# Order of the sums, the transposes and the right logits in each TensorE slot of an edge stage

## What is computed

```python
feat_src_e = feat_all[edge_type, edge_src]          # a gathered row of 256 features per edge
el = sum(feat_src_e * attn_l[edge_type])            # left logit, 4 heads
er = sum(feat_dst_e * attn_r[edge_type])            # right logit, from the destination's tile
e = leaky_relu(el + er)
ex = exp(e - segment_max(e, edge_dst)[edge_dst])    # softmax over the edges of a node
alpha = ex / segment_sum(ex, edge_dst)[edge_dst]
h = segment_sum(alpha[..., None] * feat_src_e, edge_dst)
```

## Time and profile before

| | us |
|---|---|
| median of 3 runs | 2175.03 (2172.45 to 2175.23) |
| profiled execution | 2174.1 |
| its span, first to last instruction | 2172.0 |
| first gather starts | 258.71 |
| last gather starts | 1512.77 |
| last addition of the edge stage starts | 1563.22 |

### The profile page before, as it was taken

How to read it: one execution, slowest core, us unless ns; L and a number is a source line. 1 busy time by engine, 2 the same in 40 slices (tenths; PEclk the granted TensorE clock), 3 DMA queues, 4 the chain that set the end, 5 groups by cost and what they waited for, 6 DMA issues and landing times. The chain is left out here.

```text
span 2172.0 us, 38726 instructions
## 1 busy us (share of the span) xinstructions
PE 1840.9 (85%) x9090; PEld 1554.6 (72%) x9091; DVE 1137.2 (52%) x3066; ACT 850.6 (39%) x2220; POOL 1140.9 (53%) x1130
## 2 busy tenths in 40 slices
PE   7999867888888887988888888887552999999998
PEld 6888766766767776766766766676352888888887
DVE  4333145767666677767767676776773121212121
ACT  2222354444444454544544544542083222222222
POOL 4000177777777777777777777776056122222222
PEclk9999857788788798888888888887855999999999
DMA  6443344444444444444444444443144777777764
GB/s 222 167 188 143 142 112 110 112 114 112 110 113 110 111 112 112 112 113 109 112 113 110 112 112 110 112 108 97 44 161 150 233 218 234 222 224 223 227 217 130
DMA packets 120198, 308.99 MB, mean 142 GB/s; under 512 B 26951, under 2 KB 70855, under 8 KB 105828
## 3 DMA queue, kind: packets, MB, share of 16 engines
q0 software_dynamic: 60192, 149.24, 26.7%
q1 hardware_dynamic: 59844, 158.18, 21.3%
HBM read 250.66 MB, written 57.71 MB: 142 GB/s over the span
## 5 line engine op out<-in xcount | busy, mean ns | idle before, releaser
L716 POOL DMA_INDIRECT gath<-feats,idxT x996 | 951.7, 956 | 512.6 <-issue 295.0
L1014 PE MATMUL psP<-gath,hot 128*128 128x260 f32 x1992 | 614.1, 462 | 50.7 <-DVE gath L825 49.9
L1014 PEld LDWEIGHTS psP<-gath,hot 128*128 128x128 f32 x1992 | 435.0, 230 | 135.3 <-issue 47.7
L1001 PEld LDWEIGHTS psE<-er,hotT 128*128 128x128 f32 x1992 | 294.8, 227 | 122.4 <-issue 121.4
L1001 PE MATMUL psE<-er,hotT 128*128 x1992 | 309.1, 304 | 79.3 <-issue 37.7
L937 ACT COPY hotT<-psOT 128x512 f32<-128x512 f32 x249 | 144.9, 582 | 453.5 <-PE psOT L985 453.2
L927 ACT ACTIVATE hot<-cst,ndlT 128x128 f32<-128x128 f32 x996 | 317.5, 393 | 6.5 <-PEq L307 6.5
L834 DVE TENSOR_TENSOR acc<-acc,psP 128x260 f32 x498 | 210.2, 422 | 195.8 <-PE psP L1014 76.0
L1536 POOL DMA_INDIRECT out<-yrow,node x66 | 102.6, 1555 | 390.9 <-DVE yrow L1651 292.5
L825 DVE TENSOR_TENSOR gath<-gath,psA 128x1024 f32<-128x1024 f32 x249 | 301.1, 1219 | 9.9 <-ACT gath L957 2.5
L1606 ACT ACTIVATE hT<-psH,w1buf 128x256 f32<-128x256 f32 (+1 forms) x320 | 119.1, 434 | 352.2 <-PE psH L1566 352.2
(11 more groups left out here) (224 smaller groups left out, 1192.9 us busy)
## 6 DMA issues: line engine op xcount, KB each, us to landing
w1buf<-in_experts SPq DMA_DIRECT2D x40, 1030.0 KB, 7.8
w2buf<-in_experts SPq DMA_DIRECT2D x40, 1024.0 KB, 5.4
feats<-frow SPq DMA_DIRECT2D x30, 1040.0 KB, 4.0
gath<-feats,idxT POOLq DMA_INDIRECT x996
meta<-in_edges SPq DMA_DIRECT2D x464, 12.0 KB
xrow<-slots_x SPq DMA_DIRECT2D x26, 258.0 KB, 6.4
b_all<-in_b SPq DMA_DIRECT2D x40, 128.0 KB, 6.5
xs<-xb SPq DMA_DIRECT2D x5, 768.0 KB, 10.0
```

The source lines that it names most:

```text
L716: pool.indirect_dma_start(gath[:, r, u], None, feats, bass.IndirectOffsetOnAxis(ap=idxT[:, r, u:u + 1], axis=0)).then_inc(gath_in[r], 16)
L1001: ins = pe.matmul(psE[:, u * W % 512:u * W % 512 + W], hotT[:, j % 2, k * P:(k + 1) * P], tables[k // BLK], start=True, stop=True)
L1014: ins = pe.matmul(psP[:, bank(g, b, r), 0:FW], hot[:, r, u], gath[:, r, u], start=u % BLK == 0, stop=u % BLK == BLK - 1)
```

## The change

In each slot the call of `total` moves from the end to the start. Nothing is added or removed; the once-a-group work, and the order on all other engines, stay where they are. Before, a slot is transposes, right logits, sums; now it is sums, transposes, right logits.

```diff
                     def slot(s):
+                        if s < SLOTS_Q - LAG:
+                            total(g - 1, (r - 1) % GBUFS, s + LAG)
+                        else:
+                            total(g, r, s - (SLOTS_Q - LAG))
                         if s + 2 < SLOTS_Q:
                             turn(g + 1, (r + 1) % GBUFS, s + 2)
                         else:
...
                             right_logits(g + 1, s + 1)
                         if s == 5 and there(g + AHEAD):
                             meta_rows(g + AHEAD)
-                        if s < SLOTS_Q - LAG:
-                            total(g - 1, (r - 1) % GBUFS, s + LAG)
-                        else:
-                            total(g, r, s - (SLOTS_Q - LAG))
```

## The result

The changed kernel takes 2216.26 us (median of 4 runs, 2205.66 to 2221.23) against 2175.13 before (median of 4 runs taken with it): a ratio of 1.0187, 95% interval 1.0171 to 1.0204. It is slower by 41 us, where 2237 had been forecast. Its profiled execution took 2212.11 us, 38 more than the one of before, and its span is 2210.1 us.

The account below looks back on a forecast made before the run. POOL's gathers were taken to pace the edge stage at 40.3 us a group; 0.4 + 1.1 + 1.2 = 2.7 us a period, 2.3 beyond the slack, gave 63 us on 2174.1: 2237, range 2174 to 2268.

Parts of the forecast that it names:

- the slack: Edge stage: TensorE and VectorE alone take 39.9 us against POOL's pace of 40.3, so 0.4 us a period is hidden.
- Place C: `pick_right(g+1,1)`, which needs quad 7's right logits, now behind the sums of quad 1: 1.2 us a period.
- high-clock end of 0.3: Low end of the 0.3 to 1.0 us price at the pick of quad 7's right logits, TensorE at high clock.
- low-clock end of 3.4: Price at the pick of quad 7's right logits if TensorE runs at the low clock: 3.4 us.
- Place B: Ahead of L1059: transposes and right logits now come between quad 6's sums and L1059; 1.1 us a period.
- 0.35 us case: Ahead of L1059: the price if the clock has risen again by the transposes and right logits, 1.25 - 0.9.
- Place A: Ahead of L1050 and `pick_right(g+1,0)`: delay behind the sums of quad 4, set against a gain; +0.4 us a period.
- gain weighed against it: Sums of quad 3 no longer wait 1.01 us, so VectorE's wait for L1050 may shrink by up to 0.9 us a period.
- The last two periods: End of the edge stage, without POOL's cover: 5.4 us more, less 4.9 us that group 30 waited for its gather.
- range of 8 in 10: Whole kernel: the time was to lie between 2174 and 2268 us.
- case held most likely: Whole kernel: the forecast case, 2205 to 2262 us, given a chance of 0.52.
- The rival that followed the Trainium skill: TensorE's clock: short holes leave it alone, the low clock does not spread; 1.05 us a period, 2189 us, chance 0.16.

## Why the prediction was right, and where it was off

**What bounds the kernel: right.** POOL paces the stage and the slack is 0.4 us a period. The kernel with fewer gathers has an own period of 40.0 us, and every full kernel with an own period up to 40.6 us came out within 0.2% of before. (A slip without consequence: POOL's row of sevens begins with the sixth slice, not the fifth.)

**Place C, the pick of right logits: right in kind, too small.** 1.2 us a period were taken, 1.7 were measured as a wait, and 2.0 as the effect of slot 6 on top of the others. The high-clock end of 0.3 came out: 6.7 us in 27 periods with the holes filled. The low-clock end of 3.4 never came; the longest wait is 1.9, since the clock falls for the sums and rises again for the transposes. That "new holes of up to a microsecond" would appear was too little; the hole is 1.7 to 2.2 us in all periods but one. About 1.3 us of it are the transposes and right logits that now stand behind the sums. Another 0.8 is a wait ahead of the right logits of slot 4 that is gone. The trace names no cause for it; two register loads stand there, and they now run while sums are queued ahead. Such waits came to 35.0 us before and are gone from the list. TensorE's timeline of before has this one:

```profile
792.15 1.07 PE L1001 MATMUL psE<-er,hotT 128*128 x8 [0.83 <-issue]
```

**Place B, L1059: right in kind, too large.** 1.1 us were taken, 0.7 measured. The sums of quad 6 do run at the low clock (3.83 us), but in the period shown the clock rises before the transposes and right logits behind them are through, which is the 0.35 us case of the text and a part of the next. On top of the other seven slots it does not lengthen the own period.

**Place A, L1050: the number came out, the gain did not come where it was looked for.** The wait for L1050 is 0.4 us a period longer, as taken. But the gain weighed against it, up to 0.9 us off that same wait, did not come. A gain of 0.6 came at another place, VectorE's waits ahead of additions (L834), which had no term in the sum. The kernel with slots 0, 1 and 2 alone has it (122.6 down to 106.9 us) and those with slot 3 or slot 6 alone hardly (118.8 and 123.0), so it belongs to the early slots.

**The sum.** 2.7 us a period were forecast and 2.0 measured, so beyond the slack 1.6 x 27 = 43 us came instead of 62. What is off is mostly the gain ahead of additions, which had no term; place B, too large by 0.4, and place C, too small by 0.5, cancel, and that is luck. The last two periods were to cost 0.5 us net and gave 6.1: 4.9 for the wait, as priced, and 2.1 in period 30 (1563.05 - 1529.55 against 1526.14 - 1490.54), less 0.9 by which period 29 is longer without its wait. Period 30 has transposes and right logits for a short group only; that this is why it is shorter was not tried. 43.0 - 6.1 is 37, against 63 forecast. The measured 2216 lies in the range of 8 in 10 and in the case held most likely.

**A step that failed** without consequence: POOL was to be held back at the end. It never was, with a delay of 43 us, just over one period, and three buffers. So two of the signs named, a POOL that waits longer than 0.3 us for sums and a later last gather, did not come. The others did: logits that fall behind more and more, VectorE's waits for L1001 and for the exponentials, and L1059 at 718.09, 1.8 us behind `dn`.

**The rule on the clock.** The rival that followed the Trainium skill (TensorE: Matmul & The Clock Gate, Part 1: the clock falls after a stretch in which the engine idles) gave 2189. The rows spoke against it (the waits of TensorE ahead of the low stretch from 705.40 us were 0.88, 0.69 and 1.03 us long), and so do the experiments: behind holes of 1.7 to 2.2 us in a busy stretch the granted clock fell in most periods, and filling them took the loss away.

## What to carry to other kernels

Where an engine works through its instructions in the order written, one that has to wait should stand behind the work that can already be done, not ahead of it; here the right logits and transposes had filled the hole, and moving the sums ahead of them turned one hole into a wait on another engine. A hole on TensorE can cost twice, once as idle time and once as a low clock for the work behind it; if the order can't be kept, cheap transposes in the hole can pay for themselves. Judge such a move place by place: six of the eight slots together shortened the own period by 0.5 us, and one, on top of the others, cost the whole 41 us. Where another engine paces a stage, first work out the own period of the rest: a change below the slack can't be seen, and one above it is paid in every period.

## What was not expected of the hardware

TensorE was busy 8.29 of the 10.50 us up to 727.30, with a hole of 2.21 us in them, and then the granted clock was 0.50 for 3.40 us, although TensorE was busy throughout those. Fourteen transposes (1.69 us) in that place kept it at 1.00, with 1.05 us of the hole left. But the hole ahead of the sums does not decide alone. In the period whose lines stand above, with the sums at 432.63, the clock stayed at 1.00 (columns as in the earlier trace rows):

```profile
425.00:432.60 7.60, 5.93 (x41) 5.22 (x39) 5.10 (x14) 6.50 (x18) 5.77 (x7) 1.00 0.40 109
432.70:436.00 3.30, 3.30 (x21) 2.97 (x22) 2.76 (x7) 0.88 (x3) 2.54 (x3) 1.00 0.50 132
```

What tells such a period from the others isn't settled.

Between kernels the mean clock is no guide. In the profiled executions the changed kernel has 0.861 against 0.855 before, and loses 41 us; what counts is whether the low clock falls on work that another engine waits for. Between executions of one kernel it can be a guide: the four of the changed kernel took 2205.66, 2212.11, 2220.41 and 2221.23 us at mean clocks of 0.865, 0.861, 0.859 and 0.856.
